# Routing of three sequences moved from the dispatched feed-forward stage into the full attention before it

## What is computed

```
# part 6: full attention, 16 heads of 64
scores = q @ k.T / 8;  attn = softmax(scores);  x = x + (attn @ v) @ Wo.T + bo
# part 7: dispatched experts, 8 of them, each token goes to 2, each expert takes cap = 512
scores = softmax(layernorm(x) @ wg);  gates_k, idx_k = top_k(scores, 2);  gates_k /= sum(gates_k)
loc = running count of the tokens of each expert, all first choices ahead of all second ones
valid = loc < cap
disp[idx_k, loc] = layernorm(x);  out = relu(disp @ w1 + b1) @ w2 + b2
x = x + sum_k gates_k * valid * out[idx_k, loc]
```

## Time and profile before

| what | us |
| --- | --- |
| median of three executions | 1699.73 |
| the profiled execution: its time | 1704.74 |
| its span | 1702.6 |
| busy in the span: PE, DVE, ACT, POOL | 1396.4, 1069.8, 749.0, 736.8 |
| stage 6, first statistics to last addition to x | 1073 to 1546.7 |
| stage 7, statistics to end of span | 1547.0 to 1702.6 |

### The profile page before, as it was taken

One profiled execution on the slowest core, in us unless ns is written; L12 is line 12 of the kernel. 1 busy time (PEld: TensorE's weight loads), 2 busy tenths in 40 slices (PEclk: granted clock), 3 DMA queues, 4 the chain that ended last, 5 costly groups with the idle time before them and its releaser, 6 DMA issues. The chain is left out here.

```text
span 1702.6 us, 24958 instructions
## 1 busy us (share of the span) xinstructions
PE 1396.4 (82%) x8907; PEld 849.7 (50%) x8907; DVE 1069.8 (63%) x2934; ACT 749.0 (44%) x1168; POOL 736.8 (43%) x795
## 2 busy tenths in 40 slices
PE   5487689879997793899977999799999999985193
PEld 2355556644444562444435777454554545534063
DVE  5865588668884547788843322578778777756212
ACT  3554244436664143466643333365455454430041
POOL 4533245532222555322242443256546455563533
PEclk9687689859999795699988999899999999996597
DMA  2000005200000124000001020000000000003213
GB/s 91 12 8 1 27 8 212 83 1 1 1 2 1 58 62 166 1 2 1 1 1 52 1 99 1 1 1 1 1 1 1 1 1 1 1 1 124 62 50 99
DMA packets 29562, 52.74 MB, mean 31 GB/s; under 512 B 3216, under 2 KB 24592, under 8 KB 27264
## 3 DMA queue, kind: packets, MB, share of 16 engines
q1 hardware_dynamic: 26144, 44.36, 7.4%
q0 software_dynamic: 3296, 6.78, 1.2%
HBM read 29.07 MB, written 21.02 MB: 29 GB/s over the span
## 5 line engine op out<-in xcount | busy, mean ns | idle before, releaser
L2400 DVE CUSTOM_DVE_ANT_0 s_masked_scores<-s_for_max,s_mask_qk 128x128 bf16<-128x128 f32 (+3 forms) x512 | 227.1, 487 | 58.6 <-PE s_for_max L2224 56.9
L2833 POOL TENSOR_TENSOR wbuf<-s_probs 128x1024 f32<-128x1024 f32 x64 | 152.1, 2376 | 207.0 <-ACT s_probs L2992 207.0
L2992 ACT ACTIVATE s_probs<-s_scores 128x1024 f32<-128x1024 f32 x128 | 132.3, 1034 | 201.8 <-PE s_scores L2914 201.8
L2176 POOL TENSOR_SCALAR_AFFINE_SELECT s_probs<-s_probs 128x256 f32<-128x256 f32 x256 | 101.4, 409 | 269.2 <-ACT s_probs L2331 154.3
L3034 DVE TENSOR_REDUCE s_negmax<-s_for_max 128x2 f32<-128x1024 f32 x126 | 152.1, 1207 | 21.2 <-PE s_for_max L2889 21.2
L2224 PE MATMUL s_for_max<-s_k_stack,s_q_stack 32*128 32x128 f32 (+3 forms) x512 | 143.1, 440 | 25.8 <-DVE s_max_wide L2400 16.3
L3041 DVE RECIPROCAL s_recip<-s_pv_and_sums 128x128 f32<-128x128 f32 x128 | 116.7, 934 | 47.1 <-PE s_pv_and_sums L2940 47.1
L2224 PEld LDWEIGHTS s_for_max<-s_k_stack,s_q_stack 32*128 32x128 f32 x512 | 73.1, 204 | 128.4 <-DVE s_max_wide L2400 85.3
L2331 ACT ACTIVATE s_probs<-s_scores 128x1024 f32<-128x1024 f32 x128 | 127.4, 1024 | 17.9 <-PE s_scores L2245 17.6
L2927 PE MATMUL s_pv_and_sums<-s_probs,s_v 128*64 128x512 f32 x512 | 123.9, 605 | 0.9 <-DVE wbuf L3049 0.9
L2259 PE MATMUL s_pv<-s_probs,s_v_and_one 128*32 128x512 f32 (+3 forms) x1024 | 96.1, 470 | 1.5 <-DVE s_o L2419 1.5
(11 more groups left out here) (579 smaller groups left out, 3442.4 us busy)
## 6 DMA issues: line engine op xcount, KB each, us to landing
rows_by_expert<-s_empty_rows SPq DMA_DIRECT2D x8, 1032.0 KB, 10.5
s_w<-extra SPq DMA_DIRECT2D x2, 2048.0 KB, 7.3
wbuf<-w SPq DMA_DIRECT2D x1, 3460.0 KB, 11.3
s_probs<-extra SPq DMA_DIRECT2D x1, 2898.0 KB, 9.6
wbuf<-w SPq DMA_DIRECT2D x1, 2888.0 KB, 13.7
wbuf<-w SPq DMA_DIRECT2D x1, 2124.0 KB, 7.8
dispatched<-s_empty_slots SPq DMA_DIRECT2D x1, 2064.0 KB, 8.5
s_rows<-dispatched SPq DMA_DIRECT2D x8, 258.0 KB
```

The lines of the kernel that those rows point to most:

```text
L2176: last = nc.gpsimd.affine_select(out=diag, in_=diag, compare_op=ALU.is_ge, fill=0.0, base=0, pattern=[[0, diag.shape[1]], [1, P]], channel ...
L2400: last = nc.vector.tensor_tensor_reduce(out=junk[:, m % 2, at:at + n], in0=p1[m % 2][:, at:at + n], in1=mask[:, S - n:S], scale=1.0, scala ...
L2833: nc.gpsimd.tensor_tensor(added[half], probs[:, g % 2, 2 * half, :, :], probs[:, g % 2, 2 * half + 1, :, :], ALU.add).then_inc(s_added, 1)
L2992: nc.scalar.activation(probs[:, g % 2, j, :, :], p2[:, :, :], ACT.Exp, scale=dh ** -0.5).then_inc(s_exp, 1)
```

## The change

For the first three sequences everything of stage 7's routing, up to the slots of the first choices, becomes items of full_plan, placed in rounds of the next sequence: statistics in n = 2, scaling and transposes in n = 4, logits and exponential in n = 5, choice and count in n = 6. Their tiles and semaphores live in a new class, Routing, that spans both stages; the normalised rows lie in the free part of a weight buffer. The transposes, logits and counts take the odd-jobs banks. POOL makes constants ahead of its loop, takes the reciprocal deviations at n = 3, and sends each sequence's four tiles two by two after its sums of rounds n = 7 and n = 0. The choice is made anew: the largest eight of a tile's eight scores (max), then twice a match_replace per tile and a comparison, instead of ranks over pairs. Stage 7 keeps the last sequence's routing, its 4 sends and the 16 second-choice sends. The core of the diff:

```diff
+        ahead = lambda quarter: [(ROUTE_AHEAD[n, quarter], c - 1)] if now and c and (n, quarter) in ROUTE_AHEAD else []
...
-        plan += [("stats", c + 1)] * (more and n == 0) + [("scaled", c + 1)] * (more and n == 1)
+        plan += [("stats", c + 1)] * (more and n == 0) + [("scaled", c + 1)] * (more and n == 1) + ahead(0)
...
+        plan += ahead(2)
         plan += [("ln", c + 1)] * (more and n == 1) + r[2:3]
...
+ROUTE_AHEAD = {(2, 2): "r_stats", (4, 0): "r_scaled", (4, 2): "r_ln", (5, 0): "r_logits", (5, 2): "r_exp",
+               (6, 0): "r_choose", (6, 2): "r_count"}
+ROUTE_STEPS = 27
...
+class Routing:
...
+        buf, own = sh.wbuf[at % 2], sh.weights[stage][0].shape[1]
+        self.xn = buf[:, own:own + NT * row].rearrange("p (t d) -> p t d", d=row)
+        self.xT = buf[:, own + NT * row:own + NT * row + S]
+        self.wg = sh.w(stage)["wg"]
+        self.weights_in = sh.wsem[stage]
+        self.ln = LayerNorm(sh, ctx, tag, keep=self.xn[:, :, 0:D], sem_of=lambda m: ctx.enter_context(nc.semaphore(m)))
...
+    def constants(self, pool):
+        nc, U = self.nc, self.top * NT
+        nc.gpsimd.memset(self.ones[:, :], 1.0).then_inc(self.s_const, 1)
+        nc.gpsimd.memset(self.tri[:, :], 1.0).then_inc(self.s_const, 1)
+        nc.gpsimd.memset(self.run[:, 1, :], 0.0).then_inc(self.s_const, 1)
+        nc.gpsimd.iota(self.spare_i[:, :], pattern=[[P, U]], base=SLOTS7, channel_multiplier=1).then_inc(self.s_const, 1)
+        nc.gpsimd.iota(self.token_i[:, :], pattern=[[P, NT]], base=0, channel_multiplier=1).then_inc(self.s_number, 1)
+        pool.wait_ge(self.s_const, 4)
+        nc.gpsimd.affine_select(out=self.tri[:, :], in_=self.tri[:, :], compare_op=ALU.is_gt, fill=0.0, base=0,
+                                pattern=[[1, P]], channel_multiplier=-1).then_inc(self.s_const, 1)
...
+    def numbers(self, dve):
+        nc = self.nc
+        for e in range(self.n_exp):
+            nc.vector.memset(self.run[:, 0, e:e + 1], float(e * self.cap)).then_inc(self.s_base, 1)
+            nc.vector.memset(self.limit[:, e:e + 1], float((e + 1) * self.cap) - 0.5).then_inc(self.s_base, 1)
+        nc.vector.memset(self.pick[:, :, :, :], -1.0).then_inc(self.s_base, 1)
+        dve.wait_ge(self.s_number, 1)
+        nc.vector.tensor_copy(self.xn[:, :, D], self.token_i[:, :]).then_inc(self.s_number, 1)
+        dve.wait_ge(self.s_const, 5)
+        nc.vector.tensor_copy(self.spare[:, :], self.spare_i[:, :]).then_inc(self.s_number, 1)
...
+    def put(self, u):
+        self.nc.gpsimd.indirect_dma_start(self.sh.disp, bass.IndirectOffsetOnAxis(ap=self.idx[:, u:u + 1], axis=0),
+                                          self.xn[:, u % NT, :], None).then_inc(self.s_put, 16)
...
+        pe.wait_ge(self.s_xT, c + 1)
+        for i in range(TPC):
+            last = self.nc.tensor.matmul(logits[:, i, :], xT[:, i * P:(i + 1) * P], self.wg, start=True, stop=True)
+        last.then_inc(self.s_logits, 1)
...
+        pe.wait_ge(self.s_chosen, c + 1)
+        if c == 0:
+            pe.wait_ge(self.s_const, 5)
+        flat = self.chosen[:, c * TPC:(c + 1) * TPC, :, :].rearrange("p t k e -> p (t k e)")
+        nc.tensor.matmul(ps[:, 0:n], self.tri[:, :], flat, start=True, stop=False, skip_group_check=True)
+        for i in range(1, TPC):
+            nc.tensor.matmul(ps[:, i * k16:n], self.ones[:, :], flat[:, 0:n - i * k16], start=False,
+                             stop=(i == TPC - 1), skip_group_check=True)
+        for i in range(TPC):
+            last = nc.tensor.matmul(ps[:, n:n + k16], self.ones[:, :], flat[:, i * k16:(i + 1) * k16],
+                                    start=(i == 0), stop=(i == TPC - 1), skip_group_check=True)
+        last.then_inc(self.s_count, 1)
...
+        st.then(nc.vector.tensor_reduce(self.stat[:, ts], logits, AX.X, ALU.max))
+        nc.vector.tensor_tensor(self.probs[:, ts, :], logits, self.wide(self.stat[:, ts]),
+                                ALU.subtract).then_inc(self.s_less, 1)
...
+    def choose(self, dve, st, c):
+        nc, ts = self.nc, slice(c * TPC, (c + 1) * TPC)
+        mine = self.probs[:, ts, :]
+        dve.wait_ge(self.s_exp, c + 1)
+        st.then(nc.vector.tensor_reduce(self.stat[:, ts], mine, AX.X, ALU.add))
+        st.then(nc.vector.reciprocal(self.stat[:, ts], self.stat[:, ts]))
+        st.then(nc.vector.tensor_tensor(mine, mine, self.wide(self.stat[:, ts]), ALU.mult))
+        for i in range(TPC):
+            st.did(nc.vector.max(out=self.order[:, i, :], in_=mine[:, i, :]))
+        st.wait()
+        dve.wait_ge(self.s_base, 2 * self.n_exp + 1)
+        for k in range(self.top):
+            st.did(nc.vector.tensor_copy(self.pick[:, k, :, 0:1], self.order[:, :, k:k + 1]))
+        st.wait()
+        left = mine
+        for k in range(self.top):
+            for i in range(TPC):
+                st.did(nc.vector.match_replace(out=self.rest[:, k, i, :], in_to_replace=self.pick[:, k, i, :],
+                                               in_values=left[:, i, :], imm_value=-1.0))
+            st.wait()
+            taken = nc.vector.tensor_tensor(self.chosen[:, ts, k, :], self.rest[:, k, :, :], left, ALU.is_lt)
+            if k < self.top - 1:
+                st.did(taken)
+            else:
+                taken.then_inc(self.s_chosen, 1)
+            left = self.rest[:, k, :, :]
...
+        st.then(nc.vector.tensor_tensor(kept, slot_of, limit, ALU.is_lt))
+        st.then(nc.vector.tensor_tensor(kept, kept, self.chosen[:, ts, k, :], ALU.mult))
+        st.did(nc.vector.tensor_tensor(picked, kept, slot_of, ALU.mult))
+        st.then(nc.vector.tensor_reduce(self.valid[:, us], kept, AX.X, ALU.add))
+        st.did(nc.vector.tensor_reduce(self.where[:, us], picked, AX.X, ALU.add))
+        st.then(nc.vector.scalar_tensor_tensor(out=self.gate[:, us], in0=self.valid[:, us], scalar=-1.0,
+                                               in1=self.spare[:, us], op0=ALU.add, op1=ALU.mult))
+        st.then(nc.vector.tensor_tensor(self.where[:, us], self.where[:, us], self.gate[:, us], ALU.subtract))
+        return nc.vector.tensor_copy(self.idx[:, us], self.where[:, us])
...
+        dve.wait_ge(self.s_count, c + 1)
+        if c == 0:
+            dve.wait_ge(self.s_number, 3)
+        else:
+            dve.wait_ge(self.s_slots, c)
+        within = ps[:, 0:TPC * k16].rearrange("p (t k e) -> p t k e", t=TPC, k=self.top)
+        every = self.run[:, :, :].unsqueeze(1).broadcast_to([P, TPC, self.top, self.n_exp])
+        st.then(nc.vector.tensor_tensor(self.slot_of[:, ts, :, :], within, every, ALU.add))
+        nc.vector.tensor_tensor(self.run[:, :, :], self.run[:, :, :], ps[:, TPC * k16:(TPC + 1) * k16].rearrange(
+            "p (k e) -> p k e", k=self.top), ALU.add).then_inc(self.s_slots, 1)
+        self.keep(st, ts, 0).then_inc(self.s_idx, 1)
...
-        odd = [item for item in plan if item[0] in ("ln", "proj", "maxT", "v", "out")]
+        odd = [item for item in plan if item[0] in ("ln", "proj", "maxT", "v", "out", "r_ln", "r_logits", "r_count")]
...
+            if what == "r_ln":
+                return rt.s_xT, item[1] + 1
+            if what == "r_logits":
+                return rt.s_less, item[1] + 1
+            if what == "r_count":
+                return rt.s_slots, item[1] + 1
...
+            rt.constants(pool)
...
+                    if half == 0 and n == 3 and c:
+                        rt.ln.rstd_of(pool, c - 1)
...
+                if n == PAIRS - 1 and c:
+                    if c == 1:
+                        pool.wait_ge(sh.slots_cleared, 32)
+                    pool.wait_ge(rt.s_idx, c)
+                    for t in range((c - 1) * TPC, (c - 1) * TPC + 2):
+                        rt.put(t)
+                if n == 0 and c >= 2:
+                    for t in range((c - 2) * TPC + 2, (c - 1) * TPC):
+                        rt.put(t)
+            for t in range((B - 2) * TPC + 2, (B - 1) * TPC):
+                rt.put(t)
...
+                elif what == "r_ln":
+                    rt.ln.turned(pe, item[1], odd_bank(item))
+                elif what == "r_logits":
+                    if item[1] == 0:
+                        pe.wait_ge(rt.weights_in, 16)
+                    rt.route(pe, item[1], odd_bank(item), rt.xT)
+                elif what == "r_count":
+                    rt.count(pe, item[1], odd_bank(item))
...
+                elif what == "r_ln":
+                    c = item[1]
+                    act.wait_ge(rt.ln.s_T, c + 1)
+                    if c:
+                        act.wait_ge(rt.s_logits, c)
+                    nc.scalar.copy(rt.xT, pj[fills[item] % 2]).then_inc(rt.s_xT, 1)
+                elif what == "r_exp":
+                    rt.exp(act, item[1])
...
+                elif what == "r_stats":
+                    if item[1] == 0:
+                        rt.numbers(dve)
+                    dve.wait_ge(s_x, TPC * (item[1] + 1))
+                    rt.ln.stats_of(dve, item[1])
```

(86 more changed lines are left out.)

181 lines of the change are left out of this document (64 added, 117 removed).

## The result

The changed kernel takes **1705.4 us** (median of 12 runs, 1702.18 to 1707.9) where the kernel before takes 1699.8 (12 runs beside it, 1694.68 to 1704.47): a ratio of **1.0030**, 95% interval 1.0023 to 1.0038. Slower by 5.6 us, 5.4 above the forecast and inside the range; "slower by over 0.2%" came, which had 0.35. The profiled executions differ by less (spans of 1703.7 and 1702.6 us) because the stages ahead, which the change doesn't touch, happened to run 5.4 us shorter in the profiled execution of the changed kernel (first exponential of the full attention at 1093.37, against 1098.73). So the two stages are read by their own lengths.

A forecast was written before the change was run, and what follows sets the result against it. PE was taken as full in stage 6's full attention, serial routing as bounding stage 7's head. Costs 0.9 + 3.0 + 5.5 + 10.7 = 20.1 us against 20.3 gained gave 1700 us, range 1693 to 1708.

The forecast's parts named there:

- slower by over 0.2%: Whole kernel: outcome slower than before by more than 0.2% (3.4 us), chance 0.35.
- The gain in stage 7: Head of stage 7: only the last sequence is routed there, so its first send comes 20.3 us earlier.
- Statistics, scaling and transposes: Rounds n = 2 and n = 4: statistics cost 0.9 us, scaling nothing, transposes with their bank wait 3.0.
- Logits: Round n = 5: bank wait of 0.9 plus products of 0.95, three times 1.85, 5.5 us.
- Choice: Round n = 6: copies held beside POOL's addition; 3.6 us for each of two sequences, last 3.5, sum 10.7.
- each of some eight new stops of PE: Stage 6: about 0.05 us added for each new stop of PE, leaving nothing of the gain.
- DVE isn't held: Rival, round n = 6: DVE runs freely beside POOL, stage 6 pays 12.7 us, time 1692; chance 0.29.
- The head not shortened: Rival, stage 7: first send still waits, for expert weights on the same DMA engines; time 1720, chance 0.04.
- The slots caught: Rival, stage 6: slots also held by POOL's additions, +6.7 us, 1706.5, up to 1711 if held twice; chance 0.31.
- no change: Centre of the forecast: stage 6's cost cancels stage 7's gain, median about 1700 us; chance 0.36.

The follow-up runs named there:

- two kernels that took the clock's part away in different ways: Changed kernel with six unread products ahead of PE's stalled product: ratio 1.0007; changed kernel with the choice's two copies written as one-element maxima: ratio 0.9994.
- the spread kernel: Changed kernel with the routing work cut into smaller pieces, placed in rounds where engines had slack, copies written as one-element maxima: 1695.59 us, ratio 0.9932.
- the two kernels with the counts one quarter later: Changed kernel with transposes, logits and counts one or two quarters later: ratio 1.0018; the same with the copies as one-element maxima: ratio 1.0022.

## Why the prediction was right and wrong

- **The gain in stage 7** was right: 20.9 against 20.3 (range 20.1 to 20.6).
- **Statistics, scaling and transposes** were right: 0.8 and 3.2 against 0.9 and 3.0, with nothing in the last sequence, as said.
- **Logits**: the wait of 0.91 for the bank and products of 1.03 stood where forecast, 1.9 a round; in one of three the clock fell behind them, +1.7. The wait and the products were right; the fall of the clock was missed.
- **Choice**: copies held until POOL's addition ended, stall 2.46 for 2.8; without the clock the term of 3.6 a round would have been right. Each of the two rounds paid 5.9 to 6.0, because of 2.4 us at the lower clock (18.48 to 16.13 and 18.60 to 15.30 less 0.9, in two kernels that took the clock's part away in different ways). This is the step that failed: the sum priced a stall at its length, with 0.05 for "each of some eight new stops of PE". The stall of 2.46 us cost nearly twice its length (5.9 to 6.0 less the 0.8 for copies and counts). The last sequence paid 3.8 against 3.5, but that agreement is luck: 1.6 of it is the lower clock behind the wait of 1.06 shown above, and the rest comes from a held comparison (a stall of 1.52) and one held subtraction.
- **"DVE isn't held"** fell: the copies were held in the round n = 6, TENSOR_TENSOR with both sources in SBUF in the choice and the slots, TENSOR_SCALAR in n = 3 of the spread kernel. (read as additions of POOL, lie beside subtractions of it that take 1.27 to 1.29 us each, one behind the other; the reading of the hold stays.) **"The head not shortened"** fell too. **"The slots caught"** had nearly the size measured (1706.5), but in sequences 1 and 2 of the changed kernel it didn't happen, and in the last it was one subtraction; the two kernels with the counts one quarter later show that it decides as soon as the slots come late, as written, and that it then costs up to 5.3 us in a round (two holds, a stall of 3.3 and lower clock behind it), not 2.4.
- A sum of 20.1 + 2 x 2.4 + 1.7 = 26.6 comes out at 6.3 over before by the forecast's gain of 20.3, near the 5.6 measured. So the centre of the forecast, no change, was wrong. The range held by luck: its upper end came from the rival of the caught slots, not because the clock was thought of.

Open: which stalls let the clock fall. 0.95 never did (six times) and 2.07 did each time (six times). But 1.53 behind the choice didn't while 1.52 in the last sequence of the same kernel did; 2.46 did in the changed kernel and not in one round of another; 0.91 at the logits did in sequence 1 and not in 2, in both profiles of the changed kernel; and 2.66 ahead of the output products did in nine profiles and not in three. No run here separates the stall from what PE did in the rounds ahead.

## What to carry to other kernels

Before laying small work into a full engine's list, draw up for one round the free time ahead of the next product that needs each result, and the times at which POOL adds; then cut the work into pieces that fit, and give pieces that must run beside POOL a form that isn't held. Price a stall of a full TensorE twice, with and without a fall of the clock behind it: here 2.07 us cost 3.9 with the fall (2.3 when filled), 0.95 us cost 1.2 without it, and a wait of 0.91 cost 1.7 more where the clock fell. Moving one item "for free" shifts all behind it: look at the round after, too.
